# Three Newton iterations on GpSimd split over the attention steps, and four VectorE tiles issued at other places

## What is computed

```python
x = x + tanh(g_xattn) * attention(layernorm(x), ctx_1024, Wq, Wk, Wv, Wo, bo)
x = x + tanh(g_ffn) * experts(layernorm(x))

# layernorm: (x - mean) / sqrt(var + eps)
# experts: the router takes the mean over a sequence's tokens, softmax, top 2 of 8
hmid = gelu(hidden @ w1[e] + b1[e])
y = hmid @ w2[e] + b2[e]
out = out + combine[:, e] * y
```

## Time and profile before

| | us |
|---|---|
| median of three runs | 321.41 |
| the profiled execution's own time | 321.67 |
| span of its instructions | 319.7 |
| PE busy in the span | 313.2 (98%) |
| DVE busy | 236.5 (74%) |
| ACT busy | 164.6 (52%) |
| POOL busy | 84.5 (26%) |

### The profile page before, as it was taken

How to read it: one execution, slowest core, us unless ns; L and a number is a source line. 1 busy time by engine, 2 the same in 40 slices (tenths; PEclk the granted TensorE clock), 3 DMA queues, 4 the chain that set the end, 5 groups by cost and what they waited for, 6 DMA issues and landing times.

```text
span 319.7 us, 5709 instructions
## 1 busy us (share of the span) xinstructions
PE 313.2 (98%) x1861; PEld 269.9 (84%) x1861; DVE 236.5 (74%) x563; ACT 164.6 (52%) x577; POOL 84.5 (26%) x158
## 2 busy tenths in 40 slices
PE   8999999999999999999999999999999999999996
PEld 7878998878988999888788888888887899888896
DVE  1889999989989999999998475466767554442643
ACT  2648565686766768766366254444543442321320
POOL 1325547586476655425600000000000000000000
PEclk9999999999999999999999999999999999999999
DMA  7997300300000009500016250000020000000012
GB/s 261 386 330 9 35 3 1 133 1 3 0 0 3 0 2 331 195 3 0 2 8 255 79 187 0 0 0 0 24 99 11 2 0 0 2 0 0 2 66 67
DMA packets 21918, 19.99 MB, mean 63 GB/s; under 512 B 11708, under 2 KB 17540, under 8 KB 21508
## 3 DMA queue, kind: packets, MB, share of 16 engines
q1 hardware_dynamic: 21616, 19.14, 19.9%
q10 hardware_dynamic: 276, 0.52, 0.4%
HBM read 17.56 MB, written 2.11 MB: 62 GB/s over the span
## 4 chain that ended last, share of the span: by engine, by line
PE 71%; POOL 10%; DVE 7%; issue 7%; DMA 2%; ACT 2%; SPq 0%; POOLq 0%; DVEq 0%
PE ps L1153 22%; PE ps L1154 22%; PE ps L1155 22%; POOL sx L504 4%; DMA xt<-in_x_dram 2%; POOL xs L524 2%; PE ps L1238 2%; POOL xs L522 2%; ACT sx L636 1%; DVE mx L903 1%; PE ps L1173 1%; DVE pT_lo L862 1%; PE ps L1326 1%; DVE sm L873 1%; PE ps L1424 1%
## 5 line engine op out<-in xcount | busy, mean ns | idle before, releaser
L723 ACT ACTIVATE gel<-ps,b1sel 128x512 f32<-128x512 f32 x64 | 43.9, 690 | 95.5 <-PE ps L1155 95.4
L1112 DVE CAST h_hi<-gel 128x512 fp32r<-128x512 f32 x64 | 28.4, 444 | 58.8 <-ACT gel L723 58.5
L636 ACT ACTIVATE sx<-ps,mx 128x64 f32<-128x64 f32 x128 | 38.3, 325 | 26.2 <-DVE mx L903 26.1
L1153 PE MATMUL ps<-yT_hi,w_hi 128*128 128x512 f32 (+1 forms) x128 | 50.5, 395 | 0.0
L1154 PE MATMUL ps<-yT_lo,w_hi 128*128 128x512 f32 (+1 forms) x128 | 50.0, 390 | 0.0
L1155 PE MATMUL ps<-yT_hi,w_lo 128*128 128x512 f32 (+1 forms) x128 | 49.9, 390 | 0.0
L1114 DVE TENSOR_TENSOR h_lo<-gel,h_hi 128x512 fp32r<-128x512 f32 x64 | 44.9, 702 | 2.2
L504 POOL TENSOR_TENSOR sx<-sx,rs 128x512 f32<-128x512 f32 x32 | 33.5, 1066 | 41.5 <-DVE rs L878 40.8
L1153 PE MATMUL ps<-h_hi,w_hi 128*128 128x512 f32 x96 | 38.4, 400 | 0.0
L1155 PE MATMUL ps<-h_hi,w_lo 128*128 128x512 f32 x96 | 37.5, 390 | 0.0
L1154 PE MATMUL ps<-h_lo,w_hi 128*128 128x512 f32 x96 | 37.4, 390 | 0.0
(11 more groups left out here) (149 smaller groups left out, 670.3 us busy)
## 6 DMA issues: line engine op xcount, KB each, us to landing
stage_w<-in_L_ffn_w_dram SPq DMA_DIRECT2D x7, 1024.0 KB, 7.4
out_dram<-xt SPq DMA_DIRECT2D x6, 256.0 KB, 2.3
wqT<-in_L_xattn_Wq_dram SPq DMA_DIRECT2D x2, 512.0 KB, 7.2
wv_sb<-in_L_xattn_Wv_dram SPq DMA_DIRECT2D x2, 512.0 KB, 8.8
wo_sb<-in_L_xattn_Wo_dram SPq DMA_DIRECT2D x1, 1024.0 KB, 13.9
xt<-in_x_dram SPq DMA_DIRECT2D x1, 1024.0 KB, 10.6
xs<-in_xT_dram SPq DMA_DIRECT2D x1, 1024.0 KB, 11.1
spread<-x_stat SPq DMA_DIRECT2D x1, 1024.0 KB, 4.6
```

What stands on the lines that cost most here:

```text
L636: last = nc.scalar.activation(sx[:, par, c0:c0 + M], ps[:, 2 * par + 1, c0 - BANK:c0 - BANK + M], ACT.Exp, bias=mx[:, par, h:h + 1], accum ...
L723: nc.scalar.activation(gel[:, f % 4, :], ps[:, h_bank, :], ACT.Gelu, bias=b1sel[:, b, slot, f:f + 1]).then_inc(gelu_done, 1)
L1112: nc.vector.tensor_copy(h_hi[:, f % 4, :], gel[:, f % 4, :]).then_inc(hhi_ready, 1)
L1153: mm(acc, hi_w, hi_x, start=start, stop=False)
```

## The change

Three things are moved; no instruction is added or removed, and PE's, ACT's and SP's programs are as they were.

1. `newton` is split into `newton_head` (the wait for DVE's guess and the scaling) and `newton` (so many iterations). For y tiles 0 to 3 and 4 to 7, the head and one iteration now stand in steps 6 and 10 ahead of the multiplications, and the other two iterations at the end of the same step, after x_scaled. For x tiles 8 to 15, two iterations stay at the end of step 4 and the third goes into step 5, between the multiplications and x_scaled. Those of y tiles 8 to 11 stay ahead of the multiplications in step 15.
2. DVE makes y tile 0 in step 7 ahead of its two readings of the VW groups, instead of after them.
3. DVE makes y tiles 1, 2 and 3 in steps 8, 9 and 10 as before, but near the start of the step, after the statistics (and y_guess) and ahead of pT_lo, instead of at its end.

```diff
+        Y_FIRST, Y_WHILE = 7, {8: 1, 9: 2, 10: 3}
...
-            def newton(t0, t1, rstd, var, guess):
+            def newton_head(t0, t1, var, guess):
+
+                pool.wait_ge(guess_ready, guess)
+                link(nc.gpsimd.tensor_scalar(ve_p[:, 0:t1 - t0], var[:, t0:t1], -0.5, None, ALU.mult))
+
+            def newton(t0, t1, rstd, times):
...
-                for _ in range(3):
+                for _ in range(times):
...
             def step(s, par):
-                if s in (7, 11, 15):
-                    y_rstds((s - 7) // 4)
+                if s in (6, 10):
+                    y_head((s - 6) // 4)
+                    newton(*Y_PARTS[(s - 6) // 4], rstd2, 1)
+                if s == 15:
+                    y_head(2)
+                    y_rstds(2, 3)
...
+                if s == 5:
+                    newton(*X_PARTS[2], rstd1, 1)
+                    pool.sem_inc(x_rstd, 1)
                 if active(s + LEAD) and s + LEAD >= XT0:
                     x_scaled(s + LEAD)
+                if s in (6, 10):
+                    y_rstds((s - 6) // 4, 2)
...
                 if s == 4:
-                    newton(*X_PARTS[2], rstd1, ve_x, 3)
-                    pool.sem_inc(x_rstd, 1)
+                    newton_head(*X_PARTS[2], ve_x, 3)
+                    newton(*X_PARTS[2], rstd1, 2)
...
+                if s in Y_WHILE:
+                    y_tile(Y_WHILE[s])
...
+                if s == Y_FIRST:
+                    y_tile(0)
                 if s in LATE:
                     for odd in range(2):
                         group(LATE[s][0], LATE[s][1] + odd)
...
                 for y in (Y_WITH_X.get(s + 1), Y_AFTER.get(s + 1)):
-                    if y is not None:
+                    if y is not None and y > 3:
                         y_tile(y)
```

More of the change, by code:

```diff
@@ L468, in newton @@
                 tt, ts = nc.gpsimd.tensor_tensor, nc.gpsimd.tensor_scalar
-                pool.wait_ge(guess_ready, guess)
-                link(ts(v, var[:, t0:t1], -0.5, None, ALU.mult))
-                for _ in range(3):
+                for _ in range(times):
                     link(tt(u, v, r, ALU.mult))
@@ L476, in newton, with y_head, y_rstds @@
                     link(tt(r, u, r, ALU.mult))
-            def y_rstds(i):
-                newton(*Y_PARTS[i], rstd2, ve_y, len(X_PARTS) + i + 1)
+            def y_head(i):
+                newton_head(*Y_PARTS[i], ve_y, len(X_PARTS) + i + 1)
+            def y_rstds(i, times):
+                newton(*Y_PARTS[i], rstd2, times)
                 pool.sem_inc(y_rstd, 1)
             def step(s, par):
-                if s in (7, 11, 15):
-                    y_rstds((s - 7) // 4)
+                if s in (6, 10):
[4 more added lines that the diff above has]
+                    y_rstds(2, 3)
                 t = s + LEAD
@@ L505, in step @@
                                                 ALU.mult).then_inc(mul_done, 1)
+                if s == 5:
+                    newton(*X_PARTS[2], rstd1, 1)
+                    pool.sem_inc(x_rstd, 1)
                 if active(s + LEAD) and s + LEAD >= XT0:
                     x_scaled(s + LEAD)
+                if s in (6, 10):
+                    y_rstds((s - 6) // 4, 2)
                 if s == 1:
-                    newton(*X_PARTS[1], rstd1, ve_x, 2)
+                    newton_head(*X_PARTS[1], ve_x, 2)
+                    newton(*X_PARTS[1], rstd1, 3)
                     pool.sem_inc(x_rstd, 1)
                 if s == 4:
-                    newton(*X_PARTS[2], rstd1, ve_x, 3)
-                    pool.sem_inc(x_rstd, 1)
+                    newton_head(*X_PARTS[2], ve_x, 3)
+                    newton(*X_PARTS[2], rstd1, 2)
             def x_scaled(t):
```

## The result

| | before | after |
|---|---|---|
| median, 12 runs each | 321.41 us (321.14 to 321.81) | 322.25 us (322.13 to 322.50) |
| ratio, 95% interval | | 1.0024 (1.0017 to 1.0031) |
| the profiled execution's own time | 321.67 us | 322.13 us |
| span | 319.7 us | 320.0 us |

The change makes the kernel **0.84 us slower**. The forecast was 321.0 with a range up to 321.6; the time lies outside it, on the side that I gave 0.06.

What follows compares the result with a forecast made beforehand. PE, busy 313.2 of 319.7 us, bounds the kernel, then the loop through pT_lo. PE gains 0.63, 0.29 and 0.51, gives back 0.6 and about 0.45, leaving -0.4: 321.0 against 321.41, range 320.5 to 321.6.

Steps and rivals of the forecast that it cites:

- What bounds the kernel: Whole kernel: PE's holes in steps 6 to 12, under 2.4 us, cap any gain; the DVE and ACT loop has no slack.
- Part 1: Newton for x, one iteration into step 5: step 6's 0.34 goes, scores still wait for VW; gain zero.
- Part 2: Newton for y in steps 6 and 10: step 7's multiplications start at 67.84, and 0.51 of step 12's hole goes.
- Part 3: Step 7, y tile 0 ahead of VW readings: PE's scores of step 8 start 0.63 sooner, pT_lo 0.48 sooner.
- Rival A: Step 7: tile 0 loses the race to x_scaled; 321.45, no change; chance 0.27 together with a do-nothing rival.
- Part 4: Steps 9 to 16: loop stays about 0.4 sooner; PE gives back 0.6 in step 12, about 0.45 in step 16.
- refund of tile 2: Step 9: tile 2's 0.85 at the step's end is given back to DVE, into its wait for step 10.
- Rival C: Steps 8 to 10: early tiles stall the loop if POOL is at work, +1.0, 322.4 with tile 0's loss; chance 0.06.

Runs made afterwards that it cites:

- e3: The changed kernel with y tile 0 back behind the VW readings and tiles 1 to 3 at their steps' ends, leaving only GpSimd's part; 321.57 us, ratio 1.0001.
- f1: The changed kernel, but x_scaled's first instruction in step 7 waits by semaphore until y tile 0 is made; 321.70 us, ratio 1.0003.
- e1: The changed kernel with y tile 0 put back behind DVE's two VW readings in step 7; 322.10 us, ratio 1.0019.
- f2: f1 with y tiles 1 to 3 at the ends of steps 8 to 10; 321.13 us, ratio 0.9976.
- e2: The changed kernel with y tiles 1 to 3 back at the ends of steps 8 to 10; 322.04 us, ratio 1.0018.
- g1: f2 with all of x's newton back in step 4; 320.81 us, ratio 0.9967.
- g2: g1 with y tile 2 near the start of step 9; 320.64 us, ratio 0.9967.
- f3: The changed kernel, but x_scaled's second instruction in step 9 waits for y_guess; 322.64 us, ratio 1.0025.
- e4: The kernel before with only DVE's part of the change, GpSimd's order as before; 322.15 us, ratio 1.0021.
- g3: The kernel before with only the third iteration of x's newton moved into step 5; 321.71 us, ratio 1.0000.
- f4: GpSimd's part of the change, and of DVE's only y tile 2 early in step 9; 321.57 us, ratio 1.0000.

## Why the prediction was wrong, point by point

**What bounds the kernel: right.** PE's holes are the roof, and DVE's pT_lo the second clock. In each of the eleven experiments PE's last products have the shift of pT_lo in step 17, to 0.05.

**Part 1: forecast 0, measured +0.1.** I followed its late statistics to the DMA and to the multiplications, and not what stands beside the x_scaled that it pushes back: y_guess of step 6. The holes of step 6 came out as forecast: the 0.34 before the second half went, and the scores wait for the VW reading as long as before in sum. PE of after (56.63 is 57.02 in before's time, against 57.00 in the earlier trace rows):

```profile
56.63 0.50 PE L1175 MATMUL ps<-a_hi,xT_hi 128*128 128x512 f32 x1 [0.73 <-DVE vw L831]
```

**Part 2: right, and its gain given back in the same step.** Newton's iterations were through at 67.06 and the multiplications started at 67.58 (67.97 in before's time, forecast 67.84, the 0.13 being part 1's). In e3, where DVE's order is that of before, the 0.51 of step 12 was gone, PE's second half being 0.63 ahead, and from step 13 PE was 0.2 ahead. Of the rest, only 0.12 had gone into the wait for y tile 4, to which the prediction gave 0.6; 0.30 went into the wait for yT_lo of tile 4, ahead of the transposes of tile 5 (PEld of e3), which the prediction didn't have:

```profile
103.44 0.20 PEld L1346 LDWEIGHTS ps<-ident,yb 128*128 128x128 f32 x2 [0.30 <-DVE yT_lo L995]
```

What e3 keeps comes from y tiles 0 and 4, which take 0.80 and 0.77 there instead of 1.02 and 0.91, since POOL's instructions beside them have moved. In after, where the loop came late, PE's weight loads in step 12 still stood 0.24 for the second multiplication.

**Part 3, tile 0's race: the step that failed first.** I had tile 0 ask 0.04 ahead of the multiplication's end, saw that nothing in the trace tells who wins at that distance, and gave the forecast, which has it win, 0.5. It asked 0.05 ahead and lost. Rival A was right on the mechanism and on the place of pT_lo (73.3 forecast, 73.46 measured). The one row that I took for the other outcome, y tile 4 in step 11, had been waiting for 0.7 us, not 0.04. Winning alone wouldn't have made the forecast true either. In f1, where it wins, pT_lo of step 8 is 0.19 ahead and not 0.48: 0.11 is part 1's, 0.12 is tile 0, which takes 0.40 and not 0.28, and 0.07 is tile 1. The Trainium skill, page "SBUF — State Buffer", section "Who interferes with whom", gives the lock to the one that issues first; by the recorded starts tile 0 was first by 0.09, and it lost, so the measurement decides: the recorded starts don't tell who gets it. Nor does the end of the instruction before, by which tile 0 was 0.05 ahead of the multiplication's end. What decides at such a distance stays open.

**Parts 3 and 4, the price of tiles 1 to 3: the step that failed as well.** In part 3 I charged tile 1 with 0.25, and it cost 0.31 to 0.33 (step 8: e1 less e3, f1 less f2, after less e2). The 0.25 came from L883's 0.327 less an overlap of 0.08; a y tile takes 0.40 with POOL idle (tile 1 of after at 72.76, after x_scaled's end at 71.52), and less the overlap that is 0.32. In part 4 I charged tile 3 with 0.25 and held that the rest of step 10 "stands what stood there". f1 has just the premises of that sentence (race won, PE 0.6 ahead, residual 0.64 sooner) and loses 0.65 between residual and pT_lo, not 0.25: y_guess, which now comes earlier against x_scaled, stands for 0.23; tile 3 costs 0.33 (0.41 less an overlap of 0.08); and DVE is idle for some 0.07 more behind y_guess. These three are read from the timeline, as no run has tile 3 alone early. What I called refund of tile 2 goes into the wait for PE's product unless PE is ahead.

**Rival A: right mechanism, wrong end.** The +0.1 to which "step 9's and 10's refunds" were to bring the loop back should have been +0.8. The refund is real (the residual of step 10 has a shift of +0.04), and is spent three instructions later. **Rival C**, to which I gave 0.06 and 322.4, named the reason for the second loss, early tiles in the loop, but wanted POOL's x_scaled under each tile. It needed no such accident: even at 0.40 apiece they cost, because tiles 1 and 3 stand ahead of pT_lo in steps 8 and 10, where the loop has no slack. By my own words the loop had "no slack in itself"; most of the 0.5 follows from that, and the rest from y_guess.

**Part 4, PE keeps only the loop's shift: right**, though it takes it over in step 12 and 13 and not in step 16. PE of after had no hole in step 16, since it came there with the loop already. The forecast was to be wrong if pT_lo of step 12 moved by less than 0.2 or more than 0.6: it moved by 0.72, the wrong way.

**The chances.** That DVE's instructions were moved into the loop is in the order of the queue, and most of their price, 0.33 each, stood in the earlier trace rows. Slower had deserved far more than 0.06, as A and C don't exclude each other: both came, and their costs add.

Left open: why medians and traces differ by as much as 0.23. The median less that of before lies 0.07 to 0.23 above the shift of step 17 in after and the first eight experiments, and 0.17 and 0.23 below it in g1 and g2. What is under 0.2 therefore rests on the traces alone.

## What to carry to other kernels

An instruction that is moved ahead of a link of the critical loop costs its whole length there, however idle its engine is in sum, unless that link was waiting for another engine anyway (tile 2 in step 9); what it frees at its old place counts only if the next instruction there isn't waiting for someone else. And where one engine asks for a shared port a few hundredths of a us before the other's instruction ends, don't forecast the winner and don't leave it to chance: give the one that can wait a semaphore, here one line that turned a loss of 0.4 us into a gain of 0.3.

## What the runs showed of the hardware

- Between back-to-back GpSimd instructions a y tile got in where it had waited for some time, and didn't where it had just come. Asking 0.04 to 0.05 us ahead of the multiplication's end, tile 0 lost to the next POOL instruction in after, e2 and f3 (1.17 to 1.18 us); asking 0.3 us ahead of a boundary it got in (e4, 0.52), as did tile 4 of before at 0.7 us (0.91). Distances in between weren't tried.
- An instruction of 128x4 stands like one of 128x256: y_guess's first one takes 0.17 alone and 0.27 (g3, step 6), 0.32, 0.40, 0.51 and 0.71 (e1, f1, after and e4, step 10) beside x_scaled's second instruction. It ends 0.02 to 0.03 behind that instruction's end, where a y tile ends 0.14 to 0.16 behind.
- A y tile with GpSimd idle takes 0.40 (tile 1 in after and e1, tile 2 in f4), and so does one that is given the port by a semaphore (tile 0 in f1 and g2), not 0.33 as L883. Why L883 is shorter isn't shown.
